# A decoder block on one core: the order of the transfers on SyncE's queue in the attention pass

## The reference

```
x = layernorm(x + gated(x))                 # silu gate, the smaller half of each row zeroed, times up, down projection
x = layernorm(x + attention(x, ctx))        # 32 query heads, 8 key/value heads of 32, 375 context rows per sequence
x = layernorm(x + bf16 linear(x))           # weights unpacked from 4 bits
# attention:  scores = q k^T / sqrt(32); probs = softmax(scores, axis=-1); out = probs v; out @ Wo
```

## Time and profile before

| | us |
|---|---|
| median of three runs | 2580.15 |
| the profiled execution | 2575.51 |
| its span, first to last instruction | 2573.6 |
| TensorE busy | 2432.6 (95%) |
| VectorE / ScalarE / GpSimd busy | 1268.9 / 1043.6 / 1402.1 |
| attention pass, first to last score product | 1851.3 to 2322.1 |

### The profile page before, as it was taken

The page is one execution under the profiler, slowest core; times in us unless marked ns, Lnnn a source line. Parts: engine busy times, 40 slices in busy tenths (PEclk is TensorE's granted clock), DMA queues, the critical chain, the costliest instruction groups (busy, mean ns, idle before and its releaser), DMA issues. The chain is left out here.

```text
span 2573.6 us, 33218 instructions
## 1 busy us (share of the span) xinstructions
PE 2432.6 (95%) x12861; PEld 2123.8 (83%) x12874; DVE 1268.9 (49%) x1779; ACT 1043.6 (41%) x1531; POOL 1402.1 (54%) x626
## 2 busy tenths in 40 slices
PE   9999999999999999999999999999987777788998
PEld 9999999988999889998899988999865555555775
DVE  4762205860029720178300693445476666664665
ACT  2112235432346333373333633233376666672211
POOL 5334245855448664467554684454387776672221
PEclk9999999999999999999999999999998888898999
DMA  6565522333322343233432233799765555546773
GB/s 209 169 183 182 194 104 101 110 113 126 113 99 102 117 132 113 99 107 121 125 116 102 99 107 111 216 290 294 193 169 159 163 148 134 135 119 160 178 175 91
DMA packets 254446, 371.75 MB, mean 144 GB/s; under 512 B 126640, under 2 KB 178864, under 8 KB 254032
## 3 DMA queue, kind: packets, MB, share of 16 engines
q1 hardware_dynamic: 254288, 369.61, 47.5%
HBM read 290.15 MB, written 78.70 MB: 143 GB/s over the span
## 5 line engine op out<-in xcount | busy, mean ns | idle before, releaser
L994 POOL TENSOR_TENSOR gp_w_lo<-cy_raw,gp_w_hi 128x1024 fp32r<-128x1024 f32 (+2 forms) x299 | 721.2, 2413 | 606.4 <-ACT gp_w_hi L869 605.8
L185 PE MATMUL gp_acc<-gp_x_hi,gp_w_hi 128*128 128x448 f32 x1504 | 558.1, 371 | 2.6 <-ACT gp_row L920 2.5
L187 PE MATMUL gp_acc<-gp_x_hi,gp_w_lo 128*128 128x448 f32 x1504 | 549.7, 365 | 0.0
L186 PE MATMUL gp_acc<-gp_x_lo,gp_w_hi 128*128 128x448 f32 x1504 | 549.6, 365 | 0.0
L869 ACT CAST gp_w_hi<-cy_raw 128x1024 fp32r<-128x1024 f32 (+2 forms) x300 | 307.1, 1026 | 311.7 <-PE gp_acc L187 305.4
L1457 POOL TENSOR_TENSOR ap_e_lo<-ap_e,ap_e_hi 125x1344 fp32r<-125x1344 f32 x109 | 331.2, 3066 | 134.5 <-DVE ap_e_hi L1538 103.0
L185 PEld LDWEIGHTS gp_acc<-gp_x_hi,gp_w_hi 128*128 128x128 f32 x1504 | 282.8, 188 | 25.8 <-ACT gp_row L920 4.0
L187 PEld LDWEIGHTS gp_acc<-gp_x_hi,gp_w_lo 128*128 128x128 f32 x1504 | 282.5, 188 | 22.0
L186 PEld LDWEIGHTS gp_acc<-gp_x_lo,gp_w_hi 128*128 128x128 f32 x1504 | 282.9, 188 | 20.7
L1524 DVE TENSOR_REDUCE cy_n_max<-ap_p_s 112x2 f32<-112x750 f32 x240 | 221.1, 936 | 120.4 <-PE ap_p_s L1595 117.6
L483 DVE TENSOR_REDUCE gp_sel_unit<-gp_keys 112x4 f32<-112x2048 f32 x4 | 9.1, 2286 | 547.1 <-ACT gp_keys L881 547.1
(11 more groups left out here) (207 smaller groups left out, 4411.9 us busy)
## 6 DMA issues: line engine op xcount, KB each, us to landing
cy_raw<-in_w_gu SPq DMA_DIRECT2D x172, 512.0 KB, 3.2
cy_raw<-in_w_d SPq DMA_DIRECT2D x80, 512.0 KB, 3.5
cp_c_raw<-in_ctx_t SPq DMA_DIRECT2D x32, 750.0 KB, 6.6
cy_raw<-in_w_q SPq DMA_DIRECT2D x32, 512.0 KB, 4.6
q_scratch<-gp_q_out SPq DMA_DIRECT2D x64, 224.0 KB, 6.2
cy_qs<-q_scratch SPq DMA_DIRECT2D x64, 224.0 KB, 3.4
k_scratch<-cp_k_out SPq DMA_DIRECT2D x32, 376.0 KB
cy_ks<-k_scratch SPq DMA_DIRECT2D x64, 188.0 KB, 4.2
```

What stands on the lines that cost most here:

```text
L185: nc.tensor.matmul(out, wh, xh, start=first, stop=False)
L186: nc.tensor.matmul(out, wh, xl, start=False, stop=False)
L187: return nc.tensor.matmul(out, wl, xh, start=False, stop=last)
L994: last = nc.gpsimd.tensor_tensor(o, i, hi.bitcast(F32), ALU.subtract)
```

## The change

`put_max` is cut into its two rows, and `nm_hi`'s row is issued as soon as `nm_hi` is there (semaphore `nmh`), `nm_lo`'s when `nm_lo` is. At h = 6 both rows go ahead of `fetch_qk(n + 2, 2)`, which was ahead of them. `V_AT` goes from 5 to 7: the values of batch n + 1 are fetched behind both, still ahead of h = 7's `put_o`. The first sequence's rows, in the pass before, are waited for one by one too.

```
-    def put_max(self, sp, n):
-        p, stack = n % 2, 3 * HD
-        sp.wait_ge(self.nml, n + 1)
-        for row, src in ((stack, self.nm_hi), (stack + 1, self.nm_lo)):
-            sp.dma_start(self.qs[p][row:row + 1].bitcast(F32).rearrange("o f j m q -> o (f j m) q"),
-                         src[:].bitcast(F32)).then_inc(self.nm_put, 16)
+    def put_max(self, eng, n, i):
+
+        eng.dma_start(self.qs[n % 2][3 * HD + i:3 * HD + i + 1].bitcast(F32).rearrange("o f j m q -> o (f j m) q"),
+                      (self.nm_hi, self.nm_lo)[i][:].bitcast(F32)).then_inc(self.nm_put, 16)
...
-    V_AT = 5
+    V_AT = 7
...
-                    if h in (2, 4, 6) and n + 2 < B:
+                    if h in (2, 4) and n + 2 < B:
                         fetch_qk(n + 2, h // 2 - 1)
+                    if h == TURN_AT // KT and n + 1 < B:
+                        sp.wait_ge(nmh, n + 2)
+                        cy.put_max(sp, n + 1, 0)
+                        sp.wait_ge(nml, n + 2)
+                        cy.put_max(sp, n + 1, 1)
+                        if n + 2 < B:
+                            fetch_qk(n + 2, NQK - 2)
...
-                    if h == TURN_AT // KT and n + 1 < B:
-                        cy.put_max(sp, n + 1)
```

More of the change, by code:

```diff
@@ L850, in _ @@
                 if p == 32:
-                    cy.put_max(sp, 0)
+                    sp.wait_ge(cy.nmh, 1)
+                    cy.put_max(sp, 0, 0)
+                    sp.wait_ge(cy.nml, 1)
+                    cy.put_max(sp, 0, 1)
         def part(t, n):
```

## The result

| | before | changed |
|---|---|---|
| median | 2578.16 us | 2537.84 us (2533.28 to 2543.24) |
| ratio | | 0.984, 95% interval 0.982 to 0.987 |
| profiled execution / span | 2575.51 / 2573.6 | 2542.13 / 2540.3 |

The change is faster by 40 us. I had said 2490, with 2472 to 2525 as the range, so 88 us; less than half of it came and the time lies outside the range.

A forecast was written before the change was run, and what follows sets the result against it. Bound: TensorE's 88.4 us of waits for `nm_lo`'s row, queued behind the values, plus lost clock. Fourteen batches go from 426.3 to 337.8 us, 88.5 saved and 0.3 at batch 15; forecast 2490 us, range 2472 to 2525.

The forecast's parts named there:

- the hole moves: Rival: values, or the fourth fetch behind them, come 3 to 5 us late; 2517 us at 3.5, 2553 at 4.5; chance 0.22.
- The rows go first: Maxima's rows ahead of the third fetch land 2.2 us after issue; hole left per batch 0 to 0.8, taken as 0.1.
- The values: Step 9 of each batch: values land 9.6 us after their later issue, a hole of 1.25 us; ends 0 and 3.
- the loaded case: Values in traffic in batch 5 of the kernel before: over about 9.9 us after issue, against 8.2 alone.
- GpSimd: In batches 1 to 7 it holds the period at 24.0 us or more, delaying steps 4 to 9 by 0.9.
- The clock: Half clock goes with the hole: 22.5 us per batch instead of 24.3, if new holes stay at 3 us or less.
- Third and fourth fetch: Queries and keys for pairs 8 and 12: third hidden, cost 0; fourth just covered, 0.2 us, ends 0 and 1.5.
- The clean rival: Values land in 8.2 us even in traffic; only GpSimd's 24.0 and TensorE's 22.6 remain; 2475 to 2480 us, chance 0.2.

The follow-up runs named there:

- Experiment 8: Changed kernel with the fourth fetch of queries and keys issued at head 1 behind put_o instead of at head 0; 2509.68 us (0.974).
- experiment 9: Changed kernel with the third fetch ahead of head 5's put_o, so ahead of the rows, values still in one DMA; 2490.97 us (0.966).
- experiment 4: Changed kernel with the values fetched as 112 and 13 rows instead of one DMA of 125; 2486.59 us (0.964).
- experiment 2: Kernel before with only V_AT moved from 5 to 7; the rows stay behind the third fetch; 2496.47 us (0.968).
- experiment 3: Kernel before, in its old order, with the values fetched as 112 and 13 rows instead of 125; 2505.44 us (0.972).
- experiment 6: Changed kernel with GpSimd's weight slices halved, one half in each of 16 batches, values still in one DMA; 2546.34 us (0.988).
- experiment 1: Changed kernel with V_AT back at 5: rows ahead of the third fetch, values not moved; 2543.64 us (0.987).

## Why the prediction was wrong

The direction held, and the rows' part of the mechanism. The time of the values was mis-sized, and the assumption on the clock was wrong. What came is the case that I had called "the hole moves" and given 0.22.

*The rows go first: right.* Forecast landing 2.2 us and 0.1 us left per batch; measured 2.1 and 1.6 us in all.

*The values: the step that failed.* I took 9.6 us from their issue to their landing, from the loaded case of the kernel before, so a hole of 1.25 us per batch, and named 3 us as the end for denser neighbours. Measured from issue to TensorE's going on it was 10.2 to 12.8 us, 12.0 in the median. My estimate of 9.9 for the last packet in the kernel before was right to the tenth; what I missed is 1.4 us for the denser neighbours and the 0.5 to 1.1 between the last packet and TensorE's going on, and I had rounded 0.3 down. This is the changed kernel's queue at the end of batch 2:

```profile
1933.35 0.59 SPq L149 DMA_DIRECT2D cy_qs<-cy_nm_hi  x1
1933.99 0.58 SPq L149 DMA_DIRECT2D cy_qs<-cy_nm_lo  x1
1934.62 0.59 SPq L145 DMA_DIRECT2D cy_qs<-q_scratch  x1
...
1937.53 0.48 SPq L1390 DMA_DIRECT2D ap_vs<-v_scratch  x1
1938.06 0.67 SPq L1398 DMA_DIRECT2D o_scratch<-cy_o_ab  x1
1938.77 0.72 SPq L1400 DMA_DIRECT2D cy_den<-cy_o_ab  x1
1939.54 0.49 SPq L145 DMA_DIRECT2D cy_qs<-q_scratch  x1
...
1941.87 0.66 SPq L1398 DMA_DIRECT2D o_scratch<-ap_o_ab  x1
1942.58 0.71 SPq L1400 DMA_DIRECT2D cy_den<-ap_o_ab  x1
1943.34 0.48 SPq L145 DMA_DIRECT2D cy_qs<-q_scratch  x1
```

TensorE goes on with the values here at 1949.94, 12.4 us after the issue. Behind the values SyncE issues without a pause an output, a fetch, an output and the next fetch, in 7.5 us, and the load of weights after them; before, the place behind them had SyncE's waits in it. Experiment 8 and the packets show that this company is the cause: 16.7 us of 33.3 go with one fetch moved away. I had seen the denser neighbours, and put the value at the row that was nearest by name and not by load.

*GpSimd: the right engine, half the size.* I had 0.9 us in step 4 of batches 1 to 7, laid over the wait for the values as if the longer of the two were the price. It was some 1.8, and in eight batches, since the slice of batch 7 is felt in batch 8. Laying one over the other was right: in batches 2 and 6, with a wait of 1.8 us for `e_lo`, TensorE went on with the values 12.8 and 12.6 us behind the batch's first product, in batches 10 and 12, without one, 13.2 and 12.8. So the 13.3 us for `e_lo` and most of VectorE's 4.9 are time that TensorE would else have spent waiting for the values, and the whole 51.5 us hang on the one term above. The floor of batches 1 to 8 was not 24.0: experiment 9, with nothing else in the way, has 24.6 to 24.9, with GpSimd idle for 1.08 us in the period shown, before the `e_lo` of head 4; for all its gaps I had left 0.2.

*The clock: the assumption that failed.* From rows 2 I took it that holes of 3 us or less leave the clock up. In batch 2 TensorE stood for 1.82 us, worked for 4.7 and stood for 2.56, and the clock fell to 1.2 GHz in the second hole; over batches 1 to 14 the mean granted clock is 0.93, and some 19 us of the ledger are its. It doesn't take two holes, nor one near 3 us. In batch 3 of experiment 4 there is one hole, and the clock falls behind it (the stretches have the columns of the earlier trace rows):

```profile
1928.27 0.42 PE L1637 MATMUL ap_p_o<-ap_e_lo,cy_vs 125*66 125x448 f32 x1 [1.87 <-POOL ap_e_lo L1465]
```
```profile
1928.50:1929.50 1.00, 1.00 (x7) 0.82 (x7) 0.43 (x1) 0.23 (x1) 1.00 (x1) 1.00 1.08 300
1930.00:1933.00 3.00, 3.00 (x11) 2.25 (x9) 1.89 (x3) 2.57 (x4) 3.00 (x2) 0.50 1.04 281
```

Five of that run's eight batches with such a hole lose the clock so, and take 25.4 to 25.7 us; the other three keep it and take 24.7. In experiment 2 holes of 1.55 to 1.75 us did it in four batches. On the other side stand 3.01 us in rows 2 and 3.17 in batch 7 of experiment 3, with a clock of 1.00. So the length of a hole alone doesn't tell; what does is not shown by these runs. The Trainium skill ("TensorE: Matmul & The Clock Gate", section "What's actually happening") says that the gate is set "based on how busy the PE has been recently"; the trace agrees as far as it goes, 3.17 us kept the clock and 1.87 didn't.

*Third and fourth fetch*: right, no wait of pair 8 or 12 for them. The clean rival (2475) needed the values on all engines and the weights in halves: 2475.19.

Over batches 1 to 14 forecast and profile lie 49.6 us apart: 30.1 in the holes ahead of and at step 9, 0.2 for the rows, and 19.3 by the clock. The whole profiled execution is 55.4 us above its forecast; of the other 5.8, 4.5 were lost before batch 1. There the granted clock was at its lower level for 13.7 us ahead of the pass, in the kernel before for 3.4; over all runs here it is 0 to 13.7 us, and the pass begins at 1848 to 1857, with most time lost where the clock was low for longest. No run ties this to the edit.

## What to carry to other kernels

Ask how many DMA engines a transfer gets before you ask where it stands in the queue: 125 rows in one DMA held five engines for some 7 to 12 us, and of the orders tried only those of experiments 2 and 9 let both it and the rows be nearly in time; as 112 and 13 rows it was nearly in time in every place tried. When two parts of a change lean on each other, time each alone: here one number of the change was worth 82 us and the change as a whole 40. Ask of holes that stand ahead of the same wait which of them is the limit: shortening one of the others gives nothing back (experiment 6). And the clock is to be priced for short holes too.

## What the runs showed of the hardware

- A transfer issued behind another one slows it, across engines: the values fill their five engines nearly without a gap and still take 370 ns a packet in the changed kernel, 303 when a later fetch was issued one head later (experiment 8), 272 nearly alone.
- Between the end of the last packet and TensorE's going on lie 0.5 to 1.1 us.
- TensorE's clock fell after single holes of 1.55 to 1.87 us (experiments 2 and 4) and not after one of 3.01 or 3.17 (experiment 3). The first product after a hole doesn't tell: in experiment 1 one after 3.46 us took 0.47, as at full clock, and the mean of the 6 us behind it was 0.72:

```profile
1964.00:1970.00 6.00, 6.00 (x23) 4.74 (x24) 3.08 (x3) 3.44 (x7) 4.83 (x2) 0.72 0.43 121
```

- Taking a wait away can fail to gain time: with 3.6 us less of waits for `e_lo` there were 19 us more for the values, and the kernel was 8 us slower (experiment 6).
